# First attention's queries and keys made once and put into 32-row blocks by transfers within SBUF; weights' high parts by ScalarE; the engines' lists ordered anew

## The reference, cut to what matters

```python
def _L0_attn_ref(x, Wq, bq, Wk, bk, Wv, bv, Wo, bo):      # the first attention
    q = jnp.einsum('bsd,hde->bhse', x, Wq) + bq[None, :, None, :]
    k = jnp.einsum('bsd,hde->bhse', x, Wk) + bk[None, :, None, :]
    v = jnp.einsum('bsd,hde->bhse', x, Wv) + bv[None, :, None, :]
    scale = np.float32(1.0 / np.sqrt(DH))                 # DH = 16
    scores = jnp.einsum('bhqe,bhke->bhqk', q, k) * scale
    probs = jax.nn.softmax(scores, axis=2)
    ctx = jnp.einsum('bhqk,bhke->bhqe', probs, v)
    ctx = ctx.transpose(0, 2, 1, 3).reshape(x.shape[0], x.shape[1], H * DH)
    return ctx @ Wo + bo
...
h = _L0_tok_ref(x, ...)
h = h + _L0_attn_ref(_layernorm(h, axis=-1), ...)
h = h + _L0_ffn_ref(_layernorm(h, axis=-1), ...)          # the second attention
```

## Time and profile before

| | before |
|---|---|
| median of 3 runs | 5198.48 us (5197.77 to 5199.89) |
| the profiled execution's own time | 5189.76 us |
| its span, first to last instruction | 5188.0 us |
| busy PE, DVE, ACT, POOL, shares of the span | 97%, 90%, 85%, 66% |
| chain that ended last, by engine | PE 52%, DVE 35%, issue 11% |
| transfers, share of the DMA engines | 7.7% |

### The profile page before, as it was taken

How to read it: one execution, slowest core, us unless ns; L and a number is a source line. 1 busy time by engine, 2 the same in 40 slices (tenths; PEclk the granted TensorE clock), 3 DMA queues, 4 the chain that set the end, 5 groups by cost and what they waited for, 6 DMA issues and landing times.

```text
span 5188.0 us, 196660 instructions
## 1 busy us (share of the span) xinstructions
PE 5021.8 (97%) x61744; PEld 4268.3 (82%) x61744; DVE 4664.9 (90%) x14799; ACT 4402.2 (85%) x17537; POOL 3434.1 (66%) x3462
## 2 busy tenths in 40 slices
PE   3999999999999999999999999999999999999998
PEld 3788888888888888888888888888888888888886
DVE  6899999999999999999999999999999999999996
ACT  2788888888888888888888888888888888888886
POOL 1666666666666666666666666666666666666665
PEclk8999999999999999999999999999999999999999
DMA  2000000000000000000000000000000000000000
GB/s 90 20 26 22 22 29 22 22 29 22 22 23 28 22 22 29 22 22 29 22 22 23 29 22 22 29 22 22 29 22 22 22 29 22 22 29 22 22 25 6
DMA packets 69030, 131.44 MB, mean 25 GB/s; under 512 B 8628, under 2 KB 34624, under 8 KB 68704
## 3 DMA queue, kind: packets, MB, share of 16 engines
q1 hardware_dynamic: 68960, 130.54, 7.7%
HBM read 111.14 MB, written 19.37 MB: 25 GB/s over the span
## 4 chain that ended last, share of the span: by engine, by line
PE 52%; DVE 35%; issue 11%; DVEq 1%; ACT 0%; POOL 0%; POOLq 0%; ACTq 0%
PE bank L528 42%; PE bank L705 9%; DVE nmax L948 6%; DVE nmax L1047 4%; DVE qkn L1042 4%; DVE v L1024 2%; DVE gfac L1013 2%; DVE qk L943 2%; DVE x L918 2%; DVE oT L1065 2%; DVE h L970 1%; DVE stats L905 1%; DVE ctxT L1060 1%; DVE vs L960 1%; DVE parts L921 1%
## 5 line engine op out<-in xcount | busy, mean ns | idle before, releaser
L512 POOL TENSOR_TENSOR pq<-pq,gn 99x788 f32<-99x788 f32 x768 | 1151.9, 1500 | 756.0 <-DVE gn L1056 742.4
L773 ACT ACTIVATE p<-bank,nmax 99x197 f32<-99x197 f32 x3072 | 1283.5, 438 | 219.4 <-DVE nmax L948 219.4
L811 ACT ACTIVATE pq<-bank,nmax 99x197 f32<-99x197 f32 x3072 | 1287.3, 447 | 137.8 <-DVE nmax L1047 137.8
L1047 DVE TENSOR_REDUCE nmax<-bank 99x2 f32<-99x394 f32 x1536 | 829.8, 561 | 131.0 <-PE bank L528 131.0
L516 POOL TENSOR_TENSOR sq<-qkc 128x396 f32<-128x396 f32 x768 | 644.5, 846 | 364.1 <-ACT qkc L785 364.0
L948 DVE TENSOR_REDUCE nmax<-bank 99x2 f32<-99x394 f32 x1536 | 821.3, 564 | 41.7 <-PE bank L528 38.7
L817 ACT ACTIVATE pT<-bank 99x394 f32<-99x394 f32 x1536 | 740.5, 526 | 66.0 <-PE bank L705 65.9
L528 PE MATMUL bank<-x2T,wqkc 128*128 128x198 f16 (+1 forms) x7680 | 734.1, 249 | 5.7 <-ACT p L773 4.7
L528 PEld LDWEIGHTS bank<-x2T,wqkc 128*128 128x128 f16 (+1 forms) x7680 | 654.8, 98 | 79.6 <-DVE x2T L980 41.0
L705 PE MATMUL bank<-ident,pq 99*99 99x99 f32 (+1 forms) x6144 | 709.6, 254 | 9.0 <-POOL pq L512 7.7
L811 ACT ACTIVATION_READ_ACCUMULATOR pq<-bank,nmax 99x1 f32 x3072 | 700.7, 228 | 0.0
(11 more groups left out here) (155 smaller groups left out, 10335.6 us busy)
## 6 DMA issues: line engine op xcount, KB each, us to landing
xa<-in_xa SPq DMA_DIRECT2D x128, 392.0 KB, 3.1
xb<-in_xb SPq DMA_DIRECT2D x128, 392.0 KB, 3.7
out_tokens<-res SPq DMA_DIRECT2D x128, 74.2 KB
out_tokens<-res SPq DMA_DIRECT2D x128, 73.5 KB
p<-in_wq SPq DMA_DIRECT2D x1, 1152.0 KB, 9.2
pT<-in_wk SPq DMA_DIRECT2D x1, 1152.0 KB, 11.0
qkc<-in_basis SPq DMA_DIRECT2D x2, 288.0 KB
sq<-in_wq SPq DMA_DIRECT2D x1, 576.0 KB, 6.7
```

The source lines that it names most:

```text
L512: nc.gpsimd.tensor_tensor(pair, pair, factor, op=ALU.mult).then_inc(s_sc.up(), 1)
L773: last = nc.scalar.activation(p1[0:TC, h, c, :], psum("s1", h)[0:TC, c * T:c * T + T], ACT.Exp, bias=nmax1[:, c, h:h + 1], accum_out=sum1[ ...
L811: last = nc.scalar.activation(pq[0:TC, h % SLOTS, c, 0:T], psum("s2", h)[0:TC, c * T:c * T + T], ACT.Exp, bias=nmax2[:, h, c:c + 1], accum ...
L1047: V.tensor_reduce(nmax2[:, h, :], psum("s2", h)[0:TC, 0:2 * T].rearrange("p (a b) -> p a b", a=2), op=ALU.max, axis=AX.X, negate=True).the ...
```

## The change

Four things change.

1. `qk1` on PE makes query and key of four heads in one go: the weights hold 64 columns of queries and 64 of keys for each group, so there are 5 matmuls for a group instead of 10. ACT writes one high part and DVE one low part of 128 x 198 into a new tile `qkhl`.
2. A new step `qx` on SP, once an image and after group 2, copies from `qkhl` into the 32-row blocks of `qk1`: 16 transfers of 16 rows, each with its semaphore count. `s1` on PE waits for all of them; `qk1` on ACT waits until those of the image before have landed and its scores are made.
3. Ahead of the loop ACT makes the high parts of the weights (`high_parts`), DVE the low parts as each high part is ready. One weight load less, and a clearing of `v2` moves ahead of the first wait.
4. All five lists are in a new order.

```diff
 ORDER = {
     "pe": """
-2:s1_8@6725 0:o2_0@0 0:o2_1@1 0:rstd5@4 1:qk4@3 1:qk5@6 3:x1T@4 0:s2_8@72 0:s2_10@30 1:ms0@6 2:ctx1@5 1:ms1 1:ms2
...
+1:rstd3@3 1:v2_2@5 1:v2_3@2 2:x2T@3 1:s2_2@06 1:s2_4@15 2:qk0@4 0:proj@3 1:s2_6@62 1:pT_0@7 1:rstd4@4 1:pT_1@1 2:qk1@0
+1:pT_2@4 1:pT_3@5 1:s2_8@76 2:qk2@1 3:s1_0@3024 4:tok@5 2:qk3@7 1:rstd5@0 1:pT_4@3 1:pT_5@6 3:s1_4@3152 2:qk4@7
...
     "sp": """
-4:load 0:store
+4:load 3:qx 0:store
...
+            def qk_blocks(img, _):
+
+                sp.wait_ge(*read_out(img, "qk1", 2))
+                for j in range(GROUP):
+                    for half in range(2):
+                        dst = slice(32 * j + 16 * half, 32 * j + 16 * half + 16)
+                        sp.dma_start(qk1[dst, :, 0:2, :], qkhl[16 * j:16 * j + 16]).then_inc(s_qx[j].up(16), 16)
+                        sp.dma_start(qk1[dst, :, 2, :], qkhl[64 + 16 * j:80 + 16 * j, :, half, :]).then_inc(s_qx[j].up(16), 16)
...
             def qk1_(img, g):
-                for s in range(2):
-                    w = slice(128 * (3 * s + g), 128 * (3 * s + g) + 128)
-                    last = mm5(o[:, s * TP:s * TP + TP], lambda k, r: wqk1[r, k, w], lambda k, r: x1T[r, k].rearrange("p c n -> p (c n)"), True)
+                w = slice(128 * g, 128 * g + 128)
+                last = mm5(o[:, 0:TP], lambda k, r: wqk1[r, k, w], lambda k, r: x1T[r, k].rearrange("p c n -> p (c n)"), True)
...
             def s1(img, h):
-                pe.wait_ge(*read_out(img, "qk1", h // GROUP))
+                for j in range(GROUP):
+                    pe.wait_ge(*s_qx[j].at(img, 64))
...
         def _(act):
+            def high_parts(source, dest):
+
+                nc.scalar.activation(dest[:, 0:2], source[:, 0:2], ACT.Copy, scale=W_SCALE)
+                nc.scalar.activation(dest[:, 3], source[:, 2], ACT.Copy, scale=row_scale[:, 0:1]).then_inc(s_high, 1)
...
             def split(source, dest):
-                link(V.tensor_scalar(dest[:, 0:2], source[:, 0:2], W_SCALE, None, ALU.mult))
-                link(V.tensor_scalar(dest[:, 3], source[:, 2], W_SCALE, bias_rows[:, 0:1], ALU.mult, ALU.mult))
-                link(V.scalar_tensor_tensor(dest[:, 2], source[:, 0], W_SCALE, dest[:, 0], ALU.mult, ALU.subtract))
-                link(V.scalar_tensor_tensor(dest[:, 3], source[:, 2], W_SCALE, dest[:, 3], ALU.mult, ALU.subtract))
+                high[0] += 1
+                dve.wait_ge(s_high, high[0])
+                V.scalar_tensor_tensor(dest[:, 2], source[:, 0], W_SCALE, dest[:, 0], ALU.mult, ALU.subtract)
+                V.scalar_tensor_tensor(dest[:, 3], source[:, 2], W_SCALE, dest[:, 3], ALU.mult, ALU.subtract)
```

More of the change, by code:

```diff
@@ L146 @@
     "pe": """
-2:s1_8@6725 0:o2_0@0 0:o2_1@1 0:rstd5@4 1:qk4@3 1:qk5@6 3:x1T@4 0:s2_8@72 0:s2_10@30 1:ms0@6 2:ctx1@5 1:ms1 1:ms2
[L148 to L151, removed]
+3:x1T@1 0:s2_10@20 0:o2_3@4 1:ms0@5 1:ms1 2:ctx0@3 2:ctx1@7 1:ms2 2:ctx2@6 3:qk1_0@4 3:v1@3 0:pT_8@7 3:qk1_1@1
@@ L155 @@
-1:s2_0 3:ctx0 1:s2_1 1:rstd3 0:ol4 2:nx2 3:qk1_1 1:v2_1 1:v2_2 1:rstd4 3:qk1_2 0:ol5 1:v2_3 1:s2_2 2:x2T 3:s1_4 1:s2_3
-1:gl 3:s1_5 1:gate1 1:gate2 1:gate3 3:s1_6 3:cl0 1:gr0 3:s1_7 1:s2_4 1:s2_5 1:gr1 4:tok 1:s2_6 1:s2_7 4:nx1 1:gr2
-0:proj 3:s1_8 3:s1_9 3:s1_10 1:rstd5 3:s1_11 3:ctx1 1:ol0 1:s2_8 1:s2_9 4:x1T 3:ctx2 1:gr3 1:ol1 1:s2_10 3:cl1
+0:gr4 0:s2_11 3:x1T 0:ol3 2:cl0 2:cl1 1:var2 0:gr5 2:cl2 1:rstd0 3:qk1_0 1:rstd1 1:rstd2 3:qk1_1 2:wo 1:s2_0 1:s2_1
+2:nx2 1:v2_1 1:rstd3 0:ol4 1:v2_2 0:ol5 1:v2_3 2:x2T 1:gl 1:s2_2 1:s2_3 1:gate1 1:gate2 1:gate3 1:gr0 1:s2_4 3:qk1_2
@@ L158 @@
+1:s2_5 1:gr1 1:s2_6 1:rstd4 1:s2_7 1:gr2 0:proj 1:s2_8 1:s2_9 3:s1_0 3:s1_1 3:s1_2 1:gr3 3:s1_3 4:tok 1:rstd5 3:s1_4
+3:s1_5 3:s1_6 4:nx1 1:ol0 1:ol1 3:s1_7 3:s1_8 1:ol2 3:s1_9 2:v2_0 3:ctx0 3:s1_10 3:s1_11 1:s2_10 3:ctx1 3:ctx2
 """,
     "act": """
-0:pT_2 0:pT_3 2:s1_8 2:s1_9 2:s1_10 0:o2_0 1:qk4 2:s1_11 1:qk5 0:o2_1 3:x1T 0:s2_8 0:s2_9 2:ctx1 1:var0 1:var1 0:pT_4
-0:s2_10 3:qk1_0 2:ctx2 0:pT_5 0:s2_11 3:v1 0:pT_6 0:o2_2 0:pT_7 0:pT_8 3:s1_0 0:o2_3 3:s1_1 3:s1_2 0:pT_9 0:pT_10
-0:pT_11 3:s1_3 0:o2_4 0:o2_5 1:s2_0 3:qk1_1 4:xhi 1:s2_1 3:qk1_2 2:x2T 1:s2_2 3:s1_4 3:ctx0 1:gate0 1:s2_3 2:qk0
@@ L163 @@
-3:s1_5 2:qk1 3:s1_6 2:qk2 3:s1_7 1:s2_4 1:s2_5 1:pT_0 2:qk3 1:pT_1 1:s2_6 1:s2_7
+0:o2_0 0:pT_7 0:o2_1 2:s1_6 0:o2_2 2:s1_7 2:s1_8 1:qk5 2:s1_9 2:s1_10 2:s1_11 3:x1T 0:s2_10 0:o2_3 2:ctx0 2:ctx1
+1:var0 1:var1 0:s2_11 3:qk1_0 3:v1 2:ctx2 0:pT_8 0:pT_9 3:qk1_1 0:pT_10 0:pT_11 0:o2_4 1:s2_0 0:o2_5 1:s2_1 2:x2T
+4:xhi 3:qk1_2 1:gate0 1:s2_2 2:qk0 1:s2_3 1:s2_4 1:s2_5 1:pT_0 1:s2_6 1:pT_1 1:s2_7 2:qk1 1:pT_2 1:pT_3 1:s2_8 1:s2_9
+3:s1_0 3:s1_1 3:s1_2 2:qk2 1:pT_4 2:qk3 3:s1_3 1:pT_5 3:s1_4 3:s1_5 2:qk4 1:pT_6
@@ L271, in build_vit_block @@
         bp2 = sb("bp2", [TC, D])
+        row_scale = sb("row_scale", [128, 1])
         minus_low = sb("minus_low", [128, 1])
@@ L288, in build_vit_block @@
         x1T = sb("x1T", [128, 4, 2, TC], F16)
-        qk1 = sb("qk1", [128, 3, 2, 2, TP], F16)
+        qk1 = sb("qk1", [128, 3, 3, TP], F16)
+        qkhl = sb("qkhl", [128, 3, 2, TP], F16)
         v1 = sb("v1", [TC, 2, D])
@@ L371, in build_vit_block @@
         s_qkh = signal("qk1_high_parts", 3)
+        s_qx = [signal(f"qk1_blocks{j}", 64) for j in range(GROUP)]
         s_xa = signal("x1T_half_copied", 1)
@@ L757, in qk1_ @@
                 act.wait_ge(*made(img, "qk1", g))
-                nc.scalar.activation(qk1[:, g, 0, 0, :], psum("qk1", g)[:, 0:TP], ACT.Copy, scale=E1 ** -0.25 / W_SCALE)
-                nc.scalar.activation(qk1[:, g, 0, 1, :], psum("qk1", g)[:, TP:2 * TP], ACT.Copy,
-                                     scale=mask1[:, 0:1]).then_inc(s_qkh.up(), 1)
+                for j in range(GROUP):
+                    act.wait_ge(*s_qx[j].at(img, 0))
+                if not isinstance(img, int) or img > 0:
+                    for h in range(H - GROUP, H):
+                        act.wait_ge(*made(img - 1, "s1", h))
+                nc.scalar.activation(qkhl[:, g, 0, :], psum("qk1", g)[:, 0:TP], ACT.Copy, scale=E1 ** -0.25 / W_SCALE).then_inc(s_qkh.up(), 1)
             def v1_(img, _):
@@ L832, in _ @@
             V.memset(parts[1][:], 1.0)
-            for x in (vs1, ctxT, pq, oT, xh, xl):
+            for x in (vs1, ctxT, pq, oT, xh, xl, v2):
                 V.memset(x[:], 0.0)
```

65 lines of the change are left out of this document (40 added, 25 removed).

## The result

| | before | after |
|---|---|---|
| median of 5 runs each | 5198.48 us (5196.02 to 5200.69) | 6385.45 us (6384.27 to 6391.94) |
| the profiled execution's own time, its span | 5189.76, 5188.0 us | 6391.94, 6389.9 us |

The change makes the kernel slower by 22.9%: ratio 1.2287, 95% interval 1.2271 to 1.2304. The forecast was 5430 us (range 5175 to 5610). Direction and place were right; the size was too small by a factor of five (+1187 us, +232 forecast).

A forecast was written before the change was run, and what follows sets the result against it. PE's issue was taken as the bound, 39.32 us a turn. After: 27.4 + 5.8 + 8.0 = 41.2, so 5189.76 + 233 (124 turns) + 8 - 10 = 5421, forecast as 5430 us with the 8.7 to the median; range 5175 to 5610.

The forecast's parts named there:

- What bounds the kernel, and where the new wait stands: PE's issue sets the 39.32 us turn; after the change PE waits about 3.6 us at `s1`, heads 0 to 3.
- The transfers, 8.0 us: SP's 16 transfers: 15 issue steps of 0.42 us, 6.3, plus 1.7 for landing; bounds 6.3 to 10.0.
- The clock: Rival, 12%: PE's clock falls in the wait at `s1`, at least 0.76 us a turn, +94, 5525 us.
- the forecast case: Transfers lengthen the turn to 41.2 us, 5430 us in all; 57%, alone 5300 to 5560.
- The new chain, 5.8 us: From PE's end of `x2T` through ACT's and DVE's copies, `gl`, maxima and gates to `qk1`, part 2: 5.8 us.
- PE's list, 27.4 of it behind `s1`: PE's list needs 37.6 us a turn, 10.2 from `x2T` to `s1`, 27.4 from `s1` to the next `x2T`.
- The rival that the transfers are hidden: All 16 land in 4.4 us, PE sets the pace, turn 38.2, about 5060 us; hidden or nearly, 18%.
- Ahead of the loop: DVE's preparation loses twenty instructions, some 11 us with gaps; after added work and waits for ACT, -10 us.
- The fill: While the pipeline fills, PE has little else to do in the first image's transfers: +8 us.
- DVE late to the copy: Rival, 9%: DVE reaches the `x2T` copy late; 5550 us with half the excess, 5680 with all.
- A: Theory stated after the measurement: 16 issues in one queue, 0.64 us each, set the turn; the clock falls in their wait.
- B: Rival theory stated after the measurement: the new lists are slow by themselves, the transfers only stand in front of it.

The follow-up runs named there:

- HBM run: The changed kernel with its 16 transfers reading a constant input in HBM of the same size and shape in place of `qkhl`: 6032.21 us.
- two queues: The changed kernel with eight of the 16 transfers (second half of each block) issued by ACT, the other eight by SP: 6034.33 us.
- filler run: The changed kernel with 64 useless matmuls on PE ahead of the transfer wait at `s1`, heads 0 to 3, bank waits moved ahead too: 6112.31 us.

## Why the prediction was wrong

- *What bounds the kernel, and where the new wait stands:* right. PE waits in each turn at `s1`, heads 0 to 3, for the transfers, and the chain closes through `x2T`, the gates and `qk1`, part 2, as summed.
- *The transfers, 8.0 us:* the step that failed. They take 12.01. Of the 4.0 missing, 3.3 are the issue: 0.639 instead of 0.42, beyond the upper bound of 0.46, since all its rows were transfers with HBM on one side. The HBM run shows 0.467 for the same target and bytes, so the bound was about right for what it was read from. The rest is 2.43 instead of 1.7 behind the last issue: 1.9 to the landing and 0.5 from there to `s1`, for which the sum had no term; the upper bound there, 3.1, held.
- *The clock:* taken as a rival at 12% and 0.76 us a turn "at least"; it came on top of the forecast case, not in place of it, and cost 1.87. The price was read from eight transposes, but all that stands behind the wait runs at half speed for 3 to 6 us. At the 3.6 us of the forecast it would most likely have fallen too: it did in a wait of 3.87 in the HBM run, and in or right behind one of 2.99 with two queues.
- *The new chain, 5.8 us:* 6.76. `glog` took 1.44 more beside POOL's `xl`; the rest of the chain was 0.5 shorter than its rows. The gate steps, read as 2.32 from the earlier trace rows, held such a stall already: `gfac` took 0.79 there, beside a POOL instruction and ending with it (rows below), and 0.16 in after. The move of `xlo` in POOL's list stood in the diff; what POOL does beside DVE in the chain was left out of the sum.
- *PE's list, 27.4 of it behind `s1`:* 28.28 at the upper clock, 0.9 more. In it PE waits for ACT's `pT` and DVE's `oT`, 0.79 and 0.32 us in the filler run (65.4 and 53.6 us in all in after); the first is new, the second came in place of the 0.40 us gap that was to go. Ahead of `s1` the list took 12.1 us instead of 10.2 (3042.24 to 3054.38); that shortened PE's wait, not the turn.
- *Per turn:* 4.0 + 1.0 + 1.9 + 0.9 = 7.8 us too little (7.7 by the table); with 1.88 forecast, the 9.60 measured.
- *The rival that the transfers are hidden* (5060) was priced by the work of PE and DVE alone. With them hidden and nothing stretched the turn is 39.23, not 38.2: two waits, for ACT and DVE, take up what the matmuls left free.
- *Ahead of the loop:* -10 forecast, -10 measured by itself. The fill came to some 22 to 24 us instead of 8, by difference (1202 - 1190 + 10, or + 12, POOL's wait being 12 shorter).
- *DVE late to the copy:* the rival did not come. ACT's half copy ends at 3042.77 in the turn shown and DVE's begins at 3042.98, and PE waits for `x2T`'s result once in the whole run, 1.1 us.

Timeline of DVE and POOL before, `gfac`:

```profile
2527.73 0.79 DVE L1013 SCALAR_TENSOR_TENSOR gfac<-gpair,gx 99x4 f32<-99x4 f32 x1
...
2527.65 0.84 POOL L516 TENSOR_TENSOR sq<-qkc 128x396 f32<-128x396 f32 x1 [1.99 <-ACT qkc L785]
```

A is thus shown: starting the transfers earlier took 1034 of the 1187 us away. B holds for the rest: another 181 went when `xl` was moved to where DVE reads PSUM. The two don't simply add up: with the transfers where the change has them, moving `xl` alone won 46. What stays open is why an issue takes longer with its source in SBUF; and the order of the four waits for banks was not tried by itself.

## What to carry to other kernels

A step cut into many small transfers costs the issuing queue their number times the issue time, and that time must be read from transfers between the same memories; start them where a whole stretch of other work lies ahead of their reader, before thinking of fewer or of more queues. A stall of one engine that ends exactly with an instruction of another, without a semaphore between them, moves with that instruction: look for a place where the two use different memories, and for such a stall in the rows that a forecast is read from. A wait on PE is priced with the half-speed stretch behind it.
